# A fused graph transformer block on one NeuronCore: the mixer's reciprocal roots go from VectorE to GpSimd, and three of a pair's four gathers get a wait each

## What is computed

```python
xn = _layernorm(x)
x = x + gnn(xn, node types, edge types, src, dst) + mixer(xn)
x = x + ffn(_layernorm(x))
```

```python
msg = _layernorm(msg @ Wm, g1, b1)
h = relu(concatenate([x, msg], -1) @ W1) @ W2
msg = _layernorm(h, g2, b2)
```

## Time and profile before

| | us |
|---|---|
| median of three executions | 2493.29 |
| lowest and highest | 2482.85, 2499.56 |
| the profiled execution's own time | 2516.34 |
| its span, first to last instruction | 2515.1 |
| GpSimd's first and last gather of the edge stage | 562.9, 2017.3 |

### The profile page before, as it was taken

How to read it: one execution, slowest core, us unless ns; L and a number is a source line. 1 busy time by engine, 2 the same in 40 slices (tenths; PEclk the granted TensorE clock), 3 DMA queues, 4 the chain that set the end, 5 groups by cost and what they waited for, 6 DMA issues and landing times.

```text
span 2515.1 us, 37705 instructions
## 1 busy us (share of the span) xinstructions
PE 2004.9 (80%) x10414; PEld 1497.7 (60%) x10414; DVE 1656.9 (66%) x4109; ACT 1482.5 (59%) x5053; POOL 1178.0 (47%) x1207
## 2 busy tenths in 40 slices
PE   6999997985788888888888887888888564822999
PEld 5865554553667666776676666676666443611666
DVE  8867765543778787877787787787778454626121
ACT  6745554552567776677677777677767574620222
POOL 0033334336556665566665666565655403661231
PEclk9999999997999998999999999899999887955999
DMA  5867778997788887788888888788888827841121
GB/s 185 308 232 314 311 315 273 345 364 223 230 255 263 262 269 250 252 262 263 262 268 257 263 270 255 241 256 258 255 260 235 179 45 240 276 166 30 48 58 33
DMA packets 271666, 587.06 MB, mean 233 GB/s; under 512 B 45058, under 2 KB 185672, under 8 KB 264802
## 3 DMA queue, kind: packets, MB, share of 16 engines
q0 software_dynamic: 93936, 387.70, 47.2%
q1 hardware_dynamic: 177522, 196.94, 24.7%
HBM read 407.93 MB, written 176.99 MB: 233 GB/s over the span
## 4 chain that ended last, share of the span: by engine, by line
PE 41%; DVE 21%; issue 13%; another core or an unknown queue 9%; ACT 8%; DMA 5%; DVEq 2%; SPq 2%; POOL 0%; POOLq 0%; ACTq 0%
PE bank L771 7%; PE bank L947 6%; ACT arena L1314 6%; PE bank L936 4%; PE bank L1104 4%; PE bank L1115 4%; PE bank L750 3%; DVE arena L1916 3%; DVE arena L2002 2%; DVE arena L1926 2%; DMA arena<-chunk_rel 2%; PE bank L917 2%; DVE arena L1973 2%; PE bank L619 2%
## 5 line engine op out<-in xcount | busy, mean ns | idle before, releaser
L2291 POOL DMA_INDIRECT arena<-table,arena x880 | 860.4, 978 | 604.0 <-PE bank L947 286.9
L1314 ACT ACTIVATE arena<-arena 128x64 f32<-128x64 f32 x3520 | 858.2, 340 | 0.1
L947 PE MATMUL bank<-arena 128*128 128x260 f32 x1760 | 481.7, 412 | 135.5 <-issue 76.7
L947 PEld LDWEIGHTS bank<-arena 128*128 128x128 f32 x1760 | 334.1, 201 | 243.6 <-issue 161.9
L1916 DVE TENSOR_TENSOR arena<-bank,arena 128x512 f32<-128x512 f32 x440 | 301.0, 686 | 192.8 <-remote 141.7
L936 PE MATMUL bank<-arena 128*128 128x256 bf16 x2640 | 346.0, 281 | 18.3 <-DVE arena L1916 12.7
L936 PEld LDWEIGHTS bank<-arena 128*128 128x128 bf16 x2640 | 266.4, 101 | 86.2 <-DVE arena L1916 13.2
L1926 DVE TENSOR_REDUCE arena<-arena 128x16 f32<-128x1024 f32 x220 | 267.7, 1217 | 17.3 <-issue 0.2
L771 PE MATMUL bank<-arena 64*128 64x512 f32 x832 | 211.0, 623 | 21.4 <-DVE arena L1660 15.9
L2002 DVE TENSOR_TENSOR arena<-arena,bank 128x260 f32 x440 | 184.4, 419 | 40.8 <-PE bank L947 19.8
L1198 ACT COPY arena<-bank 128x512 f32<-128x512 f32 x260 | 149.1, 595 | 87.5 <-PE bank L771 80.6
(11 more groups left out here) (315 smaller groups left out, 3020.9 us busy)
## 6 DMA issues: line engine op xcount, KB each, us to landing
arena<-q_parts SPq DMA_DIRECT2D x440, 192.0 KB
arena<-chunk_rel SPq DMA_DIRECT2D x220, 128.0 KB
arena<-table,arena POOLq DMA_INDIRECT x880
node_rows<-arena SPq DMA_DIRECT2D x24, 512.0 KB, 7.2
xl_and_sum<-arena SPq DMA_DIRECT2D x8, 1536.0 KB
arena<-in_x SPq DMA_DIRECT2D x12, 512.0 KB, 8.7
xn<-arena SPq DMA_DIRECT2D x12, 512.0 KB, 8.7
xT<-arena SPq DMA_DIRECT2D x12, 512.0 KB, 8.2
```

What stands on the lines that cost most here:

```text
L947: ins = TE.matmul(bank[b][:, 0:AW], lhsT=so[p % 2][:, c % 2, j, :], rhs=values_of(c, j), start=j == 0, stop=j == HALF - 1)
L1314: ins = A.activation(seg, seg, ACT.Copy, scale=rows[:, C + h:C + h + 1])
L2291: G.indirect_dma_start(rows_of_pair(p, i % 2 * HALF + j), None, d_tab_rows[0:N * R, :], bass.IndirectOffsetOnAxis(ap=idxE[:, g, j, c:c + 1 ...
```

## The change

- VectorE's place `nrm` and its 11 operations go. GpSimd makes the roots with a function `roots_of(g)`, called before the gathers of pair 9g + 2 (and for the last group behind the loop where it isn't reached). GpSimd has no operation with a scalar and two tensors here, so a Newton round is four operations and the whole is 14, each waiting for the one before. It waits for the same squares and raises the same `norm_ready`.
- Of the four gathers of a pair p from 13 on, the second waits for VectorE's second product of step p - 3, the third for the score of step p - 3, the fourth for the targets made in step p - 3 (from step 9 on). The first keeps its waits.
- Three places move: TensorE's `w2b` from 0 to 1 and `w1c` from 13 to 14, and ScalarE's `re0` from 13 to 14. With `nrm` gone VectorE has three places. All others stay.

```diff
-PE_AT = (0, 1, 3, 5, 7, 9, 11, 13, 13, 15, 17)
-ACT_AT = (1, 1, 5, 7, 9, 11, 13, 15)
-DVE_AT = (2, 4, 8, 11)
+PE_AT = (1, 1, 3, 5, 7, 9, 11, 13, 14, 15, 17)
+ACT_AT = (1, 1, 5, 7, 9, 11, 14, 15)
+DVE_AT = (2, 4, 11)
+ROOTS_AT, MIX_PAIRS = 2, 9
...
+GATHER_LEAD = 3
...
-                yield from until(g, nrm)
-                n_before = len(mtiles(g - 1)) if g else 0
-                if g < MG:
-                    V.wait_ge(wm_squared, g + 1)
-                if g:
-                    V.wait_ge(y2_squared, g)
-                lo_, hi_ = (0 if g < MG else MT), (MT + n_before if g else n)
-                t = step(V.tensor_scalar(var[:, lo_:hi_], sq_sum[:, lo_:hi_], 1.0 / C, LN_EPS, ALU.mult, ALU.add))
-                t = rsqrt(var[:, lo_:hi_], rstd[:, lo_:hi_], nt_tmp[:, lo_:hi_], t, last=norm_ready)
...
+        def pace(at_step, part):
+            if part == 1:
+                b, k = psum.at("q", 2 * at_step + 1)
+                G.wait_ge(empty[b], k)
+            elif part == 2:
+                G.wait_ge(scored, at_step + 1)
+            elif part == 3 and at_step >= WEIGH_LAG:
+                G.wait_ge(targets_made, at_step - WEIGH_LAG + 1)
+
+        def roots_of(g):
+            n, n_before = (len(mtiles(g)) if g < MG else 0), (len(mtiles(g - 1)) if g else 0)
+            lo_, hi_ = (0 if n else MT), (MT + n_before if g else n)
+            v, y, tmp = var[:, lo_:hi_], rstd[:, lo_:hi_], nt_tmp[:, lo_:hi_]
+            if n:
+                G.wait_ge(wm_squared, g + 1)
+            if g:
+                G.wait_ge(y2_squared, g)
+            t = step(G.tensor_scalar(v, sq_sum[:, lo_:hi_], 1.0 / C, LN_EPS, ALU.mult, ALU.add))
+            G.wait_ge(pool_step, t)
+            t = step(G.tensor_scalar(y.bitcast(i32), v.bitcast(i32), -0.5, float(0x5F3759DF), ALU.mult, ALU.add))
+            for i in range(3):
+                G.wait_ge(pool_step, t)
+                t = step(G.tensor_tensor(out=tmp, in0=y, in1=y, op=ALU.mult))
+                G.wait_ge(pool_step, t)
+                t = step(G.tensor_tensor(out=tmp, in0=tmp, in1=v, op=ALU.mult))
+                G.wait_ge(pool_step, t)
+                t = step(G.tensor_scalar(tmp, tmp, -0.5, 1.5, ALU.mult, ALU.add))
+                G.wait_ge(pool_step, t)
+                ins = G.tensor_tensor(out=y, in0=y, in1=tmp, op=ALU.mult)
+                if i < 2:
+                    t = step(ins)
+            ins.then_inc(norm_ready, 1)
+
         for p in range(NPAIR):
+            if p >= ROOTS_AT and (p - ROOTS_AT) % MIX_PAIRS == 0 and (p - ROOTS_AT) // MIX_PAIRS <= MG:
+                roots_of((p - ROOTS_AT) // MIX_PAIRS)
...
+                    if p >= VALUES_LIFE:
+                        pace(p - GATHER_LEAD, i % 2 * HALF + j)
                     G.indirect_dma_start(rows_of_pair(p, i % 2 * HALF + j), None, d_tab_rows[0:N * R, :],
...
+        for g in range((NPAIR - 1 - ROOTS_AT) // MIX_PAIRS + 1, MG + 1):
+            roots_of(g)
```

More of the change, by code:

```diff
@@ L504, in build @@
     centred, wm_squared, y2_squared = sem("centred"), sem("wm_squared"), sem("y2_squared")
+    pool_step = sem("pool_step")
     acc_cleared = sem("acc_cleared")
@@ L1834, in mix @@
             until = half_steps()
-            elu, ap, nrm, bas = DVE_AT
+            elu, ap, bas = DVE_AT
             V.wait_ge(mixw_in, 16 * 7)
@@ L1872, in mix @@
                         ins.then_inc(empty[b], 1)
-                yield from until(g, nrm)
-                n_before = len(mtiles(g - 1)) if g else 0
-                if g < MG:
-                    V.wait_ge(wm_squared, g + 1)
-                if g:
-                    V.wait_ge(y2_squared, g)
-                lo_, hi_ = (0 if g < MG else MT), (MT + n_before if g else n)
-                t = step(V.tensor_scalar(var[:, lo_:hi_], sq_sum[:, lo_:hi_], 1.0 / C, LN_EPS, ALU.mult, ALU.add))
-                t = rsqrt(var[:, lo_:hi_], rstd[:, lo_:hi_], nt_tmp[:, lo_:hi_], t, last=norm_ready)
                 if g:
                     yield from until(g, bas)
+                    n_before = len(mtiles(g - 1))
                     V.wait_ge(norm_ready, g + 1)
@@ L2223, in pool_program, with step @@
     def pool_program():
+        n_step = 0
+        def step(ins):
+            nonlocal n_step
+            ins.then_inc(pool_step, 1)
+            n_step += 1
+            return n_step
         G.iota(iota_row, [[1, P]], base=0, channel_multiplier=0, allow_small_or_imprecise_dtypes=True).then_inc(numbers, 1)
```

## The result

The kernel after takes 2546.4 us (median of 4 runs, 2541.7 to 2557.8) beside 2492.5 us before (4 runs, 2482.9 to 2499.6): a ratio of 1.0216, with a 95% interval of 1.0171 to 1.0261. The forecast was 2462 us, 1.2% faster; the change costs 54 us. The profiled execution took 2557.8 us, so it stands 11.4 us above the median, as the one of before stood 23.8 above its own.

What follows compares the result with a forecast made beforehand. No engine bounds alone: TensorE and VectorE, nearly equal, are tied by shared banks and lose time when one is late. Terms -28 + 6 + 2 + 0 - 5 - 6 = -31 us gave 2462 us, range 2415 to 2530.

Steps and rivals of the forecast that it cites:

- The root off VectorE: Edge stage: removing VectorE's 11 root operations frees its add and the scatter waiting for it; -28 us, at most 55.5.
- The root's length: GpSimd's 14 dependent operations per root: 0.30 us each, 4.2 us a root.
- The later norms: ScalarE waits 1.1 us more a group for the root, 28 us in all, a fifth felt by the scatter: +6 us.
- The gathers: Gathers queued behind GpSimd's root start 3.0 us late, fitting within 5.4 us including landing, gone three pairs on: +2 us.
- The waits before three gathers: New waits on events 3.9 to 4.2 us back seldom bind; passed waits fit GpSimd's room: 0 us.
- The places: TensorE's `w2b` and `w1c` one place later shift scatter and expansion by 1.7 us; small gain, -5 us.
- the relu: ScalarE's first relu goes behind a weighing, so its waits cover work the scatter waits for: -6 us.
- The sum: All terms together: -31 us, from the median of 2493.3 us to 2462 us, 1.2% faster.
- the largest wait: VectorE's waits for a product without a releaser in the trace, 121.5 us in 55 waits; taken as unaffected by the change.
- GpSimd's arithmetic is dear: Rival, chance 0.15: at 0.60 us an operation norms and gathers come late; +50 us, 2543 us; slower from 0.43 us.
- It is absorbed: Rival, chance 0.19: earlier VectorE just waits longer for products; only a fifth of the 28 us is left, 2488 us.
- Blocking of the two engines: Rival, chance 0.04: GpSimd operations meeting VectorE's two-input SBUF operation stand; 1.4 us more a root, +17 us, 2479 us.

Runs made afterwards that it cites:

- chip A: Label for the chip or condition in which the kernel before takes 2491 to 2493 us; the main measurement ran there.
- B: Label for the other chip or condition, in which the kernel before takes 2289 to 2297 us.
- e11: Kernel before with roots on GpSimd, VectorE also doing its 11 operations on data nobody reads; 2315.8 us, 1.0074 of the kernel before, quicker chip.
- e10: Kernel before with the root on GpSimd as one operation writing 1.0 in place of 14; 2265.0 us, 0.9859 of the kernel before, quicker chip.
- e9: Kernel before with only the 14-operation roots moved to GpSimd, old places, no new waits; 2296.3 us, 0.9998 of the kernel before, quicker chip.
- e16: Kernel before with only the roots moved to GpSimd, placed behind the pair's second gather; 1.0179 of the kernel before, quicker chip.
- e2: Kernel before with only the three waits before gathers added; 0.9980 of the kernel before, quicker chip.
- e14: Kernel before with only the roots moved to GpSimd, old places, no new waits, run again; 1.0014 of the kernel before, quicker chip.
- e13: The whole change, run on the quicker chip; 1.0028 of the kernel before.
- e4: Kernel before with the roots on GpSimd and the three waits, old places; 1.0000 of the kernel before, quicker chip.
- e7: Kernel before with the roots on GpSimd and the moved places, without the three waits; 1.0262 of the kernel before, slower chip.
- e8: Kernel before with the three waits and the moved places, roots still on VectorE; 1.0066 of the kernel before, slower chip.

## Why the prediction was wrong

**The root off VectorE, -28 us: right in size.** The first step lost 2.3 us a group on chip A. On B the eleven operations cost 19.5 us by themselves (e11), and the relief was worth 32 us with a short root, whose norms also came earlier (e10).

**The root's length, 4.2 us: right.** It measured 4.18. The page's factor, in the Trainium skill, "GPSIMD Engine Reference", section "Performance versus the Vector engine", is for large operands and gave, carried over, 5.5; the trace doesn't agree with that, with 0.28 us from one dependent four-column operation to the next beside VectorE's 0.20, a factor of 1.4 and not 1.96.

**What hangs on that length, +6 us for the later norms and +2 us for the gathers behind it: the step that failed most clearly.** The thirteen further operations of e9 cost 31 us on chip B (beside e10), where I had 8. Two readings in it were wrong.

*The later norms.* The wait was about right: ScalarE's went from 12.2 to 33.0 us on A, 21 more where 28 were forecast, and its norms start 0.9 us later. The price was not. I took "a fifth of it" as felt, because the weighing has a step of room. e16 lost 37 us for 63 us of later norms, about three times that share, a part of it perhaps by the clock.

*The gathers.* I set 3.0 us of delay against "5.4 us" of room. The delay was 4.2 us: on average the first gather of pair 9g + 2 starts 1.4 us after the score that ends step 9g - 1 in e2 and 5.6 in e14, since the root itself starts 0.9 us after that score and not with it (in 8 of the kernel after's roots it waits for ScalarE's squares, 25.3 us). The room was not 5.4 less the landing either. The DMA issues of e13 give the landing that the first trace lacked:

```profile
arena<-table,arena POOLq DMA_INDIRECT x880, 5.2
```

That is 5.2 us from issue to landing (a median over the landings that the trace records), so of my 5.4 most was landing. But the product waits for TensorE's queries too, and in e2 its rows had come 6.0 us before it on average by the packets' records, some 0.4 less by the semaphores of the landings. What I missed is that a relieved VectorE uses its room up: in e10 the product starts 1.5 us sooner after that score than in e2. The delay of 4.2 and these 1.5 us are all of the room, and the product waited 63.2 us for its rows in e14. And the delay isn't gone in three pairs: the products of the third to the sixth step all started within 1 to 2 us of their rows on average (e14). The earlier trace rows had gathers waited for once, because they had the lead then; that says nothing of how much lead.

How the 31 us fall on norms and gathers isn't shown, as no run delays one without the other. At e16's price the norms' 2.3 us between e10 and e14 would make 34 us, all of it.

**The waits before three gathers, 0: right.** e2, e4 and e7 agree; of the kernel after two waits, 16.7 us, are put down to VectorE.

**The places, -5, and the relu, -6: wrong in sign.** +10 and +15 us on B, 0.66% on A with the waits beside them. That "the scatter comes 1.7 us earlier and the next expansion no later" left out that the moved `w1c` still has to be done, and that its relu, which I had wait less, waits for exactly that product: the 13.7 us for L917 in the view of before stood beside the 90.9 that I counted.

**The sum.** With the measured terms on B it is -32 + 31 + 10 to 15, so +9 to +14 us, 0.4% to 0.6%; measured +6 (1 to 12). On chip A it was +54. The 40 us or more that are left lie in the third and fourth step, in the product's waits, 70 to 93 us longer there than before and 50 to 66 longer than in e8. Most of these end with TensorE's late results, which I had called the largest wait and then held constant: they "follow no place of the mixer, and the change removes nothing that they hang on". They did have a place: 33 of the 92 us of them in groups 3 to 22 of the first profile lay in the third step. That they grew with roots and places is shown; by what chain, and whether the roots alone would do it, stays open.

**The rivals.** The mechanism of "GpSimd's arithmetic is dear" is what happened, norms late at ScalarE and gathers late behind them, but at 0.30 us an operation and not from 0.43 on: its point of decision stood on half of ScalarE's waiting absorbed and a room of 5.4 us. "It is absorbed" is what chip B shows, for another reason than the one given. Blocking of the two engines, which had the least chance, is there and is small: each of the 18 operations of GpSimd that start beside L1968 ends just behind it. Here the trace agrees with the lock of the Trainium skill's "SBUF — State Buffer", section "SBUF: two separate sides". It took 0.3 us a root where the rival had 1.4, so it doesn't make the loss.

## What to carry to other kernels

An engine that is only 59% busy isn't free: what is inserted ahead of its DMA issues moves each of them, and the room to count is from issue to use, less the landing, and less what the relieved engine comes to the use sooner. Where the landing isn't in the trace, take it as all of the room, and not as "fits in". Work moved to another engine to relieve a shared one has two prices, its length and who waits for its result; try it with one operation in place of all, which separates what can be gained at most (32 us here) from what the length takes back (31 us). And shorten the chain before moving it.

## What was unexpected of the hardware

The same kernel takes 2491 us or 2292 us, 8% apart, with nothing changed in it. The root (4.2 us) and the scatter's matmul (412 and 404 ns in before and e13) are nearly the same. The granted clock over the span is 0.920 and 0.945; in the edge stage it stood at 1.2 GHz for 159 to 201 us on the slower chip and 51 to 121 us on the quicker, so by my estimate the clock can make at most 75 us of the 200. On the slower chip over a hundred waits of the stage end with a semaphore of TensorE that rises over 1 us after the matmul's recorded end, by up to 8.4 to 15.5 us in the six profiles, and on the quicker not one. A change that costs 0.3% on one costs 2.2% on the other, so a result of such a kernel holds for the conditions in which it was measured.

And a four-column operation of GpSimd, 0.20 us by itself, takes up to 0.73 us when it starts beside a VectorE operation with two inputs from SBUF: it ends 49 to 58 ns behind that one, in 18 cases of 18 in the kernel after. A mean over the group (199 to 212 ns) hides it.
